# Non-local attention on one core: the loads of the opening are cut and queued differently, and q's first half is handled in quarters

## The reference

```python
q = jnp.einsum('oc,bcn->bon', Wq, xf) + bq[None, :, None]
k = jnp.einsum('oc,bcn->bon', Wk, xf) + bk[None, :, None]
v = jnp.einsum('oc,bcn->bon', Wv, xf) + bv[None, :, None]
scores = jnp.einsum('bqi,bqj->bij', q, k)
attn = jax.nn.softmax(scores, axis=-1)
out = jnp.einsum('bcj,bij->bci', v, attn)
return out.reshape(B, Cc, W, H) + x
```

## Time and profile before

| | us |
|---|---|
| median of 3 runs | 170.4 |
| lowest and highest run | 170.19, 170.5 |
| the profiled execution | 170.36 |
| its span | 168.5 |

### The profile page before, as it was taken

The page is one execution under the profiler, slowest core; times in us unless marked ns, Lnnn a source line. Parts: engine busy times, 40 slices in busy tenths (PEclk is TensorE's granted clock), DMA queues, the critical chain, the costliest instruction groups (busy, mean ns, idle before and its releaser), DMA issues. The chain is left out here.

```text
span 168.5 us, 2430 instructions
## 1 busy us (share of the span) xinstructions
PE 160.3 (95%) x786; PEld 131.1 (78%) x786; DVE 138.5 (82%) x220; ACT 107.2 (64%) x196; POOL 49.7 (29%) x65
## 2 busy tenths in 40 slices
PE   7978999999999999999999999999999999999990
PEld 5567978797887898798787898798787898767870
DVE  1879899898979999899979999897979879854552
ACT  3658896836997646757896646736895636755210
POOL 6399630170235300420235300420235300214300
PEclk9999999999999999999999999999999999999999
DMA  5932465063312030251311130251311130003003
GB/s 182 352 120 78 128 196 224 0 156 83 131 44 66 28 124 0 51 138 52 124 47 57 41 126 0 55 134 47 127 48 55 42 124 0 5 0 124 0 0 126
DMA packets 7949, 14.48 MB, mean 86 GB/s; under 512 B 1672, under 2 KB 2240, under 8 KB 7936
## 3 DMA queue, kind: packets, MB, share of 16 engines
q1 hardware_dynamic: 6656, 13.37, 24.4%
q0 software_dynamic: 864, 0.82, 2.3%
q10 hardware_dynamic: 416, 0.13, 0.3%
HBM read 4.59 MB, written 4.19 MB: 52 GB/s over the span
## 5 line engine op out<-in xcount | busy, mean ns | idle before, releaser
L818 PE MATMUL acc<-w_hi,v_hi 128*128 128x512 f32 x128 | 51.2, 400 | 0.0
L818 PE MATMUL acc<-w_hi,v_lo 128*128 128x512 f32 x128 | 50.4, 393 | 0.0
L439 ACT ACTIVATE w_full<-st 128x512 f32<-128x512 f32 x64 | 37.8, 592 | 10.5 <-PE st L804 10.5
L406 ACT ACTIVATE dump<-slot,negmax 128x1024 f32<-128x1024 f32 x29 | 32.4, 1118 | 12.8 <-DVE negmax L548 12.4
L826 PE MATMUL acc<-w_lo,v_hi 128*128 128x512 f32 x120 | 38.7, 398 | 0.4 <-POOL w_lo L326 0.2
L603 DVE TENSOR_TENSOR w_lo<-w_full,w_hi 128x512 fp32r<-128x512 f32 x48 | 33.2, 693 | 5.7 <-ACT w_full L439 1.9
L548 DVE TENSOR_REDUCE negmax<-slot 128x1 f32<-128x1024 f32 x29 | 35.3, 1217 | 1.8 <-PE slot L739 1.8
L326 POOL TENSOR_TENSOR w_lo<-w_full,w_hi 128x512 fp32r<-128x512 f32 x16 | 20.7, 1291 | 47.5 <-ACT w_full L439 47.4
L818 PEld LDWEIGHTS acc<-w_hi,v_hi 128*128 128x128 f32 x128 | 24.2, 189 | 7.1 <-DVE x_sb L612 1.2
L818 PEld LDWEIGHTS acc<-w_hi,v_lo 128*128 128x128 f32 x128 | 24.2, 189 | 5.3
L826 PEld LDWEIGHTS acc<-w_lo,v_hi 128*128 128x128 f32 x120 | 22.3, 188 | 7.0 <-POOL w_lo L326 2.1
(11 more groups left out here) (84 smaller groups left out, 187.9 us busy)
## 6 DMA issues: line engine op xcount, KB each, us to landing
out<-x_sb SPq DMA_DIRECT2D x7, 512.0 KB, 2.8
x_sb<-x SPq DMA_DIRECT2D x3, 1024.0 KB, 5.5
k_b<-k_a SPq DMA_DIRECT2D x8, 192.0 KB, 2.5
q_b<-q_a SPq DMA_DIRECT2D x8, 192.0 KB, 2.6
k_a<-qk_parts SPq DMA_DIRECT2D x12, 64.0 KB, 2.2
q_a<-qk_parts SPq DMA_DIRECT2D x12, 64.0 KB, 2.3
x_sb<-x SPq DMA_DIRECT2D x1, 512.0 KB, 3.6
x_sb<-x SPq DMA_DIRECT2D x2, 256.0 KB, 4.8
```

The source lines that it names most:

```text
L406: nc.scalar.activation(dump[:, t % 2, :], s_home(b, t), ACT.Exp, bias=negmax[:, t:t + 1], accum_out=rowsum[:, t:t + 1]).then_inc(rowsum_re ...
L439: nc.scalar.activation(w_full[:, r, :], st[:, j % 2, :], ACT.Exp).then_inc(exp_done, 1)
L818: nc.tensor.matmul(acc[:, c, :], v[:, b % 2, j, ch], w_hi[:, r, :], start=(j == 0 and v is v_hi), stop=False)
```

## The change

`wqk`, `bias` and `bv` become one array `small` of 132 floats a partition: the weights of k and of q once (2 x 64), the two bias columns, and bv. ACT issues it as one transfer of 66 KB (128 runs of 528 B) and then x's piece c0 h1. SP issues c0 h0, c1 h0, c1 h1, then `wv`, which the host now lays out by partition (128 runs of 2 KB), and image 1. Each x piece has a semaphore of its own. DVE forms `wqk_hi` and `wqk_lo` from a broadcast view that reads every weight twice.

The split of `wv` leaves POOL: ACT rounds it right behind the fourth `x_hi`, DVE takes the remainder ahead of the first `put_k_lo`. POOL does the three `put_q_dup` in a row and then the quarters of image 1.

q's first half is handled in quarters of 256 pixels: the order on ACT is k half 0, q quarter 0, k half 1, q quarter 1, q half 1 (with a wait for the first `put_q_lo` ahead of quarter 1), on DVE k half 0, q quarter 0, k half 1, q quarter 1. `first_scores(0)` no longer needs anything of pixels 256 to 511; `first_scores(2)` does. The first `keep_busy` has 13 matmuls in place of 18.

```diff
+        Q_PARTS = (quarter(0), quarter(1), cols(1))
+        def q_home(i):
+            return qk_home(0, i // 2)[2 * CQK:3 * CQK, quarter(i) if i < 2 else cols(0)]
@@ sync
-            sp.dma_start(x_sb[:, 0, 0, :], x_v[0, :, 0, :]).then_inc(x0_in[0], DMA)
-            for h in range(2):
-                sp.dma_start(x_sb[:, 0, 1, cols(h)], x_v[0, :, 1, cols(h)]).then_inc(x0_in[1 + h], DMA)
-            sp.dma_start(wv[:, :, :], wv_t.rearrange("(t p) m -> p t m", p=P)).then_inc(wv_in, DMA)
+            for i in (0, 2, 3):
+                c, part = piece(i)
+                sp.dma_start(x_sb[:, 0, c, part], x_v[0, :, c, part]).then_inc(x0_in[i], DMA)
+            sp.dma_start(wv[:, :, :], wv_t).then_inc(wv_in, DMA)
...
-                sp.wait_ge(q_dup_put, h + 1)
+                sp.wait_ge(q_dup_put, h + 2)
@@ gpsimd
-            pool.dma_start(bv_sb[:, :], bv).then_inc(bv_in, DMA)
...
-            pool.wait_ge(x0_split, 4)
-            pool.wait_ge(wv_in, DMA)
-            nc.gpsimd.tensor_copy(wv_hi[:, :, :], wv[:, :, :]).then_inc(wv_cut, 1)
-            pool.wait_ge(wv_cut, 1)
-            nc.gpsimd.tensor_tensor(wv_lo[:, :, :], wv[:, :, :], wv_hi[:, :, :].bitcast(fp32),
-                                    ALU.subtract).then_inc(wv_split, 1)
-            pool.wait_ge(wv_split, 1)
-            put_q_dup(0)
-            pool.wait_ge(q_dup_put, 1)
+            for i in range(3):
+                put_q_dup(i)
+            pool.wait_ge(q_dup_put, 3)
             prepare_x1(0)
             pool.wait_ge(x1_split, 1)
-            put_q_dup(1)
-            pool.wait_ge(q_dup_put, 2)
@@ scalar
-            act.dma_start(wqk[:, :, :], wqk_t.rearrange("(t p) m -> p t m", p=P)).then_inc(wqk_in, DMA)
-            act.dma_start(bias[:, :], bias_qk).then_inc(bias_in, DMA)
+            act.dma_start(small_sb[:, :], small).then_inc(small_in, DMA)
+            act.dma_start(x_sb[:, 0, 0, cols(1)], x_v[0, :, 0, cols(1)]).then_inc(x0_in[1], DMA)
...
-                act.wait_ge(x0_in[max(0, i - 1)], DMA)
+                act.wait_ge(x0_in[i], DMA)
...
+            def put_q_hi(i):
+                act.wait_ge(qk_ready, i // 2 + 1)
+                if i == 1:
+                    act.wait_ge(q_lo_put, 1)
+                nc.scalar.activation(q_a[2 * CQK:3 * CQK, Q_PARTS[i]], q_home(i),
                                      ACT.Identity, bias=bias[2 * CQK:3 * CQK, 0:1]).then_inc(q_hi_put, 1)
-            act.wait_ge(bias_in, DMA)
+            act.wait_ge(wv_in, DMA)
+            nc.scalar.activation(wv_hi[:, :, :], wv[:, :, :], ACT.Copy).then_inc(wv_cut, 1)
+            act.wait_ge(small_in, DMA)
             put_k_hi(0)
+            put_q_hi(0)
             put_k_hi(1)
-            put_q_hi(0)
             put_q_hi(1)
+            put_q_hi(2)
@@ vector
+            wqk = small_sb[:, 0:CT * 2 * CQK].rearrange("p (g o r) -> p g o r", o=1, r=CQK)
+            wqk = wqk.broadcast_to([P, CT * 2, 2, CQK])
+            nc.vector.tensor_copy(twice(wqk_hi), wqk).then_inc(wqk_cut, 1)
...
+            dve.wait_ge(wv_cut, 1)
+            nc.vector.tensor_tensor(wv_lo[:, :, :], wv[:, :, :], wv_hi[:, :, :].bitcast(fp32),
+                                    ALU.subtract).then_inc(wv_split, 1)
             put_k_lo(0)
+            put_q_lo(0)
             put_k_lo(1)
-            put_q_lo(slice(0, P))
-            put_q_lo(slice(P, HALF))
+            put_q_lo(1)
             for t in range(TH):
                 row_max(0, t)
-            put_q_lo(cols(1))
+            put_q_lo(2)
@@ tensor
-                if t == 1:
+                if t == 2:
+                    pe.wait_ge(q_dup_put, 2)
                     pe.wait_ge(q_lo_put, 2)
...
-            keep_busy(18, QUARTER)
+            keep_busy(13, QUARTER)
```

More of the change, by code:

```diff
@@ L4, with nonlocal_attention @@
 from concourse import mybir
-def nonlocal_attention(nc, x, wqk_t, bias_qk, wv_t, bv, out):
+def nonlocal_attention(nc, x, small, wv_t, out):
     fp32 = mybir.dt.float32
@@ L68, in nonlocal_attention @@
         x_lo = sb("x_lo", [P, 2, CT, N], fp32r)
-        wqk = sb("wqk", [P, CT, P])
+        small_sb = sb("small_sb", [P, CT * 2 * CQK + 2 + CT])
+        bias = small_sb[:, CT * 2 * CQK:CT * 2 * CQK + 2]
+        bv_sb = small_sb[:, CT * 2 * CQK + 2:CT * 2 * CQK + 2 + CT]
         wqk_hi = sb("wqk_hi", [P, CT, P], fp32r)
@@ L76, in nonlocal_attention @@
         wv_lo = sb("wv_lo", [P, CT, C], fp32r)
-        bias = sb("bias", [P, 2])
         idle = sb("idle", [P, HALF], mybir.dt.bfloat16)
-        bv_sb = sb("bv_sb", [P, CT])
         eye = sb("eye", [P, P])
@@ L103, in nonlocal_attention @@
         slot = [ctx.enter_context(nc.psum_tensor(f"slot{i}", [P, N], fp32)) for i in range(2)]
-        x0_in = [sem(f"x0_in{i}") for i in range(3)]
+        x0_in = [sem(f"x0_in{i}") for i in range(4)]
         x1_in = sem("x1_in")
         x_in = sem("x_in")
-        wqk_in = sem("wqk_in")
+        small_in = sem("small_in")
         wv_in = sem("wv_in")
-        bias_in = sem("bias_in")
-        bv_in = sem("bv_in")
         idle_made = sem("idle_made")
@@ L303, in _, with put_q_dup @@
             pool.wait_ge(ones_put, 1)
-            pool.dma_start(bv_sb[:, :], bv).then_inc(bv_in, DMA)
[L306 to L309, removed]
+            def put_q_dup(i):
+                pool.wait_ge(q_hi_put, i + 1)
+                nc.gpsimd.tensor_copy(q_a[0:CQK, Q_PARTS[i]],
+                                      q_a[2 * CQK:3 * CQK, Q_PARTS[i]].bitcast(fp32)).then_inc(q_dup_put, 1)
             def second_blocks(b, h):
@@ L452, in put_k_hi @@
                                      ACT.Identity, bias=bias[0:2 * CQK, 0:1]).then_inc(k_hi_put, 1)
-            def put_q_hi(h):
-                nc.scalar.activation(q_a[2 * CQK:3 * CQK, cols(h)], qk_home(0, h)[2 * CQK:3 * CQK, :],
+            def put_q_hi(i):
[3 more added lines that the diff above has]
+                nc.scalar.activation(q_a[2 * CQK:3 * CQK, Q_PARTS[i]], q_home(i),
                                      ACT.Identity, bias=bias[2 * CQK:3 * CQK, 0:1]).then_inc(q_hi_put, 1)
-            act.wait_ge(bias_in, DMA)
+            act.wait_ge(wv_in, DMA)
+            nc.scalar.activation(wv_hi[:, :, :], wv[:, :, :], ACT.Copy).then_inc(wv_cut, 1)
+            act.wait_ge(small_in, DMA)
             put_k_hi(0)
+            put_q_hi(0)
             put_k_hi(1)
-            put_q_hi(0)
             put_q_hi(1)
+            put_q_hi(2)
             for t in range(TH):
@@ L500, in _, with twice @@
             nc.vector.memset(shift_parts[:, :, :].bitcast(fp32), 0.0).then_inc(zeros_put, 1)
-            dve.wait_ge(wqk_in, DMA)
-            nc.vector.tensor_copy(wqk_hi[:, :, :], wqk[:, :, :]).then_inc(wqk_cut, 1)
+            dve.wait_ge(small_in, DMA)
+            def twice(w):
+                return w[:, :, :].rearrange("p c (g d r) -> p (c g) d r", g=2, d=2)
+            wqk = small_sb[:, 0:CT * 2 * CQK].rearrange("p (g o r) -> p g o r", o=1, r=CQK)
+            wqk = wqk.broadcast_to([P, CT * 2, 2, CQK])
+            nc.vector.tensor_copy(twice(wqk_hi), wqk).then_inc(wqk_cut, 1)
             dve.wait_ge(wqk_cut, 1)
-            nc.vector.tensor_tensor(wqk_lo[:, :, :], wqk[:, :, :], wqk_hi[:, :, :].bitcast(fp32),
+            nc.vector.tensor_tensor(twice(wqk_lo), wqk, twice(wqk_hi).bitcast(fp32),
                                     ALU.subtract).then_inc(wqk_split, 1)
@@ L522, in put_k_lo, with put_q_lo @@
                     in1=k_a[0:CQK, cols(h)].bitcast(fp32), op0=ALU.add, op1=ALU.subtract).then_inc(k_lo_put, 1)
[L524 to L528, removed]
+            def put_q_lo(i):
+                dve.wait_ge(q_hi_put, i + 1)
                 nc.vector.scalar_tensor_tensor(
-                    out=q_a[CQK:2 * CQK, part], in0=qk_home(0, h)[rows, part.start - h * HALF:part.stop - h * HALF],
-                    scalar=bias[rows, 0:1], in1=q_a[rows, part].bitcast(fp32),
+                    out=q_a[CQK:2 * CQK, Q_PARTS[i]], in0=q_home(i), scalar=bias[2 * CQK:3 * CQK, 0:1],
+                    in1=q_a[2 * CQK:3 * CQK, Q_PARTS[i]].bitcast(fp32),
                     op0=ALU.add, op1=ALU.subtract).then_inc(q_lo_put, 1)
@@ L613, in finish @@
                                                in1=x_sb[:, b, c, cols(h)], op0=ALU.add, op1=ALU.add).then_inc(acc_read, 1)
-            dve.wait_ge(bias_in, DMA)
+            dve.wait_ge(wv_cut, 1)
+            nc.vector.tensor_tensor(wv_lo[:, :, :], wv[:, :, :], wv_hi[:, :, :].bitcast(fp32),
+                                    ALU.subtract).then_inc(wv_split, 1)
             put_k_lo(0)
+            put_q_lo(0)
             put_k_lo(1)
-            put_q_lo(slice(0, P))
-            put_q_lo(slice(P, HALF))
+            put_q_lo(1)
             for t in range(TH):
                 row_max(0, t)
-            put_q_lo(cols(1))
+            put_q_lo(2)
             first_cut_v()
@@ L632, in _ @@
                 split_w(n)
-            dve.wait_ge(bv_in, DMA)
             def turn(b):
@@ L748, in first_scores @@
```

(14 more changed lines are left out.)

## The result

The changed kernel takes 169.62 us (median of 7 runs, 169.53 to 169.9) where the kernel before takes 170.5 on the same chip (median of 7, 170.19 to 171.22): a ratio of 0.9928, with a 95% interval of 0.9906 to 0.9951. So the gain of 0.7% is clear of the spread, and small. The way there is another one.

What follows compares the result with a forecast made beforehand. PE was taken to bound the main loop, so the opening shifts the end: 0.46 + 0.05 = 0.5 us off the loop's start, 170.36 - 0.5 = 169.85 us. The range was 169.2 to 170.8.

Steps and rivals of the forecast that it cites:

- The view that PE bounds and the opening shifts the end: Whole kernel: PE bounds the main loop; each us by which the first row maximum moves shifts the end one for one.
- nothing of the change reaches into the loop: Main loop: the change moves no work of it and can only let it start earlier or later.
- the loop's length, 148.8 us: Sign: from the first `scores_t` to the span's end, 168.5 - 19.7 = 148.8 us must be kept, or the forecast is wrong.
- Part 1: Opening behind the projection: `put_k_hi(0)` to first maximum takes 3.29 us instead of 3.75, a gain of 0.46 us.
- K: Start of `put_k_hi(0)` on ACT: 8.09 us before the change, forecast at 8.0.
- The wait that ACT gained in the middle of it: ACT waits for the first q remainder (K+1.97) ahead of q quarter 1; claimed to cost nothing.
- Part 2: Loads and rounding ahead of K: earlier landings bring K to 8.0, a gain of 0.05 to 0.1 us.
- the new wait for `wv`: ACT rounds `wv` ahead of K: 0.63 us, fitting the 0.62 it waited for PE; if `wv` is late, k waits.
- c1 h0 "projected by 8.0": PE ahead of K: piece c1 h0 is split by about 7.5 and projected by 8.0, so PE is not late.
- The rival of the clock: PE's projection in the opening: matmuls 0.43 us apart instead of 0.23, end 170.6 or 171.0; chance 0.13.
- a late c0 h1: Rival, x loads: c0 h1 lands with c1 h1, K = 8.8 to 9.2, end 170.6 to 171.0; chance 0.12.
- The sum: Start of the main loop: 0.46 + 0.05 = 0.5 us earlier, so 170.36 - 0.5 = 169.85 us.

Runs made afterwards that it cites:

- the second profile: The changed kernel, with nothing altered, run and profiled once more: 168.92 us, span 167.0.
- eight more on POOL: The changed kernel with eight more instructions, long-satisfied waits, on POOL's queue right behind the three put_q_dup: 169.81 us, ratio 0.9928.
- the one-queue kernel: The changed kernel with x piece c0 h1 moved from ACT's queue to SP's, second of four there: ratio 0.9894 (0.9857 to 0.9931).

## Why the prediction was right, and where it was not

**The view that PE bounds and the opening shifts the end** held only in half. What the opening shifts does arrive at the end: 0.94 us in the first maximum are one us in the times. But the sentence that nothing of the change reaches into the loop is the step that failed. I had named the loop's length, 148.8 us, as what would show me wrong, and it was 167.7 - 20.4 = 147.3. I had read the diff for moved work, and the loop changed by where things lie: 0.4 us by SBUF offsets, and by instruction fetches, whose place DVE's queue sets: about 0.25 at the wait for `k_a` and 0.8 in the tail.

**Part 1** was right in its size. From K to the first maximum I had 3.29 us; it is 12.40 - 9.06 = 3.34, and 11.76 - 8.42 = 3.34 in the second profile, against 3.75 before. Two terms were off and nearly cancelled: DVE started on k 0.72 us after K and not 0.80, and a q quarter cost it 0.52 us of its string and not 0.41. The wait that ACT gained in the middle of it (0.18 us ahead of q quarter 1) cost nothing. The scores are released by DVE's `k_a`, as said.

**Part 2** had the landings within 0.4 us. Forecast 5.4, 6.65 and 7.3 for c0 h1, c1 h1 and `wv`; they came at 5.6 (1.17 + 4.4), 6.25 (1.65 + 4.6) and 7.0 (2.12 + 4.9). ACT rounded `wv` at 7.18 without a pause, and then stood idle for PE: 0.52 us in the second profile and 1.27 in the first. With eight more on POOL it paused 0.23 us for `wv`, and still stood idle for PE after it. So the new wait for `wv` never bound; PE did. In three profiles at the upper level, K follows the start of the rounding of c0 h1 by the same time: 5.70 and 8.42 in the second profile, 5.42 and 8.13 with 18 matmuls ahead, and with eight more on POOL

```profile
5.39 1.67 ACT L389 ACTIVATE x_hi<-x_sb 128x512 fp32r<-128x512 f32 x3 [0.86 <-DMA x_sb<-x]
...
8.11 0.68 ACT L448 ACTIVATE k_a<-slot,small_sb 64x512 fp32r<-64x512 f32 x1 [0.17 <-PE slot L720]
```

That is 2.72 us where the forecast has 2.56 (5.44 to 8.0). The term that was too small is c1 h0 "projected by 8.0": PE does the three matmuls of c0 h1 ahead of those of c1 h0. In the second profile the remainder of c1 h0 was ready at 7.66, but its last matmul started at 7.91, and ended at 8.31. The rest of the 0.42 us is c0 h1, which landed later there.

**The rival of the clock** is what the profiled execution shows, and I had given it 0.13. The 18 matmuls of zeros before came 0.213 us apart for 256 columns, the later 24 came 0.063 apart for 128. Were PE still at the first of these paces when c0 h1 came, nine matmuls of 512 columns would come at 0.43 instead of 0.23; that was the rival. It has 0.43 us a matmul (0.42 to 0.43 measured until 8.2), k's half 0 projected at 6.1 + 6 x 0.43 = 8.7, K near 8.8 (9.06 measured), the first maximum at 8.8 + 3.29 = 12.1 (12.40). It was taken for unlikely because 2.8 us of dense matmuls (13 x 0.213) remained; that such a stretch brings the upper level was my estimate and is not shown, and in four of six profiles PE was still at the lower level at the second piece. I had set it at 170.6, or 171.0 if the 24 matmuls of zeros were slow as well; the upper end of the range rests on it and on a late c0 h1. Without the gains elsewhere it would have been 170.36 + 0.56, about 170.9.

**The sum.** In the first pair of profiles: +0.65 in the opening, -0.31 and -0.39 in the loop, -0.8 in the tail; together -0.8 where I had -0.5. The forecast of 169.85 was near for the wrong reasons. At the upper level, the opening's gain is about the one forecast: first maxima at 11.76 in the second profile (and 11.46 with 18 matmuls ahead) against 11.84 and 12.65 in the two profiles of the kernel before, which starts on its last x piece at 6.84 and 7.65.

## What to carry to other kernels

When a change of an opening is measured in tenths of a us, compare the two traces by stations before believing the total: gains and losses in places without a line in the diff can be larger than the edit. An unused tile (0.34 us here) or one idle instruction (1.0 us) is a fair control for that, and worth a try on its own. Judge fewer matmuls of zeros by the worst of several executions, not by one: with 13 in place of 18, four of six profiles were still at the lower level at the second piece (0.43 us apart) and two were not. See also what PE does in the gap that follows.

## What the runs showed of the hardware

- One instruction more on DVE's queue cost 1.0 us (168.8 to 169.83): a fetch of instructions then begins between the issue and the landing of the last output, which lands in 3.0 us instead of 2.0, by one late share of 16. Three more cost nothing there, though the step around 40 us took 2.59 us with them, against 2.40 to 2.48 where no fetch falls on the transfer of `k_a`. That the fetch holds up one of the DMA engines is the reading; what was varied is only its place.
- A block of 24 matmuls of 256 columns with `wv_hi` or `wv_lo` as the moving operand took 2.80 us at one offset in SBUF and 2.87 at the other. Which of the offsets matters, and how finely, is open.
- The granted clock on the page reads 9 tenths or more in every slice of the opening, also where the matmuls came 0.43 us apart; only the distance of the matmuls, 0.43 or 0.23 us, told the level, and that it is a level of the clock is the reading. With 13 matmuls of zeros the level rose before the second x piece in two of six profiles, though PE had done nearly the same in all of them until then. What decides between them is open.
- Two queues brought the last of four equal pieces in at 6.25 us, one queue at 6.9. SP issues a transfer in 0.45 us, so the last piece is issued that much sooner with two queues (1.65 against 2.1), and the difference is 0.65 to 0.7. One profile of the one-queue kernel stands behind this, and it does not settle whether the rest is more than a difference from run to run.
